# Moving the copy of the transposed attention weights from ScalarE to VectorE, one unit closer to its use

## The reference

```python
x = x + layernorm(attn(layernorm(x), wq, wk, wv, wo))
x = x + layernorm(ffn(layernorm(x), theta, phi, theta_noise, phi_noise))
# attn: 16 heads of 64, window 256; block j of 256 queries sees the keys of
# blocks j-1 and j with  qi + 1 <= ki <= qi + 256, softmax over them, then @ wo.T
# ffn: sqrt((x @ cos(theta + theta_noise))**2 + (x @ sin(phi + phi_noise))**2)
```

## Time and profile before

| what | value |
|---|---|
| median of 3 runs | 4396.93 us (4396.27 to 4718.36) |
| the profiled execution's own time | 4396.27 us |
| its span on the slowest core (core 6) | 4394.7 us (all cores 4368.0 to 4394.7) |
| TensorE busy | 3399.2 us, 77% of the span |
| ScalarE busy | 2266.0 us, 52% |
| VectorE busy | 1429.5 us, 33% |
| mean granted TensorE clock, core 6 | 0.818 |

### The profile page before, as it was taken

The page is one execution under the profiler, slowest core; times in us unless marked ns, Lnnn a source line. Parts: engine busy times, 40 slices in busy tenths (PEclk is TensorE's granted clock), DMA queues, the critical chain, the costliest instruction groups (busy, mean ns, idle before and its releaser), DMA issues.

```text
span 4394.7 us, 51881 instructions; the slowest of 8 cores (4368.0 to 4394.7 us)
## 1 busy us (share of the span) xinstructions
PE 3399.2 (77%) x19680; PEld 2283.5 (52%) x19808; DVE 1429.5 (33%) x3088; ACT 2266.0 (52%) x3200; POOL 111.8 (3%) x215
## 2 busy tenths in 40 slices
PE   0037978889798887979887797978888797888875
PEld 0025645556565555656554555655555565555562
DVE  2312334242433424243342414233241423324142
ACT  3437265372826537282653628274462827446281
POOL 1000000000000000000000000000000000000000
PEclk6566988879798887969788697988879798887978
DMA  6772331405133140513314150422315042241503
GB/s 211 250 250 77 128 122 63 167 29 183 58 129 120 66 164 31 181 58 132 118 70 161 58 191 20 154 96 90 145 53 192 20 154 96 92 147 50 192 10 125
DMA packets 54165, 511.26 MB, mean 116 GB/s; under 512 B 5792, under 2 KB 5920, under 8 KB 28576
## 3 DMA queue, kind: packets, MB, share of 16 engines
q0 software_dynamic: 30384, 266.35, 16.1%
q1 hardware_dynamic: 23536, 241.58, 15.9%
HBM read 465.97 MB, written 41.94 MB: 116 GB/s over the span
## 4 chain that ended last, share of the span: by engine, by line
PE 55%; ACT 24%; issue 9%; DVE 8%; DMA 4%; DVEq 0%; POOL 0%; ACTq 0%; SPq 0%; POOLq 0%
PE pb L516 31%; PE pb L461 16%; ACT L742 11%; ACT L711 4%; ACT attnT_sb L742 4%; PE pb L769 3%; ACT attn_sb L711 3%; DMA wsc<-pl 2%; PE pb L669 1%; DVE stats L697 1%; PE pb L401 1%; DVE ao_sb L807 1%; PE pb L731 1%; DVE attn_sb L700 1%; DVE sc L841 1%
## 5 line engine op out<-in xcount | busy, mean ns | idle before, releaser
L769 PE MATMUL pb<-v_sb,attnT_sb 128*128 128x64 f32 x2880 | 600.1, 365 | 422.5 <-ACT attnT_sb L742 421.5
L769 PEld LDWEIGHTS pb<-v_sb,attnT_sb 128*128 128x128 f32 x2880 | 541.0, 273 | 558.4 <-issue 556.8
L697 DVE TENSOR_REDUCE stats<-pb 128x1 f32<-128x384 f32 (+2 forms) x512 | 269.8, 527 | 1397.6 <-PE pb L669 1397.3
L742 ACT ACT_TABLE_LOAD x512 | 656.9, 1283 | 16.9 <-PE pb L731 8.0
L461 PE MATMUL pb<-fmh,slot0h 128*128 128x256 bf16 x1024 | 280.2, 274 | 264.8 <-DMA slot0l<-wsc 264.8
L414 ACT ACT_TABLE_LOAD x32 | 41.1, 1283 | 793.0 <-PE pb L401 793.0
L711 ACT ACT_TABLE_LOAD x256 | 328.4, 1283 | 99.2 <-DVE attn_sb L700 95.3
L516 PE MATMUL pb<-slot2h,fmh 128*128 128x512 bf16 x961 | 364.2, 379 | 14.2 <-ACT ao_sb L898 13.4
L516 PE MATMUL pb<-slot2l,fmh 128*128 128x512 bf16 x976 | 369.9, 379 | 1.6
L516 PE MATMUL pb<-slot2h,fml 128*128 128x512 bf16 x977 | 370.3, 379 | 0.8
L731 PE MATMUL pb<-eyef_s,attn_sb 128*128 128x128 f32 x1440 | 345.6, 364 | 0.8 <-ACT attn_sb L711 0.8
(11 more groups left out here) (115 smaller groups left out, 4939.1 us busy)
## 6 DMA issues: line engine op xcount, KB each, us to landing
slot0h<-wsc SPq DMA_DIRECT2D x33, 2048.0 KB, 11.3
slot1h<-wsc SPq DMA_DIRECT2D x33, 2048.0 KB, 12.8
slot0l<-wsc POOLq DMA_DIRECT2D x33, 2048.0 KB, 14.0
slot1l<-wsc POOLq DMA_DIRECT2D x33, 2048.0 KB, 15.0
slot2h<-wsc SPq DMA_DIRECT2D x33, 2048.0 KB, 12.2
slot2l<-wsc POOLq DMA_DIRECT2D x33, 2048.0 KB, 14.4
x_sb<-x POOLq DMA_DIRECT2D x32, 512.0 KB, 6.1
y<-sc POOLq DMA_DIRECT2D x32, 512.0 KB, 3.4
```

The lines of the kernel that those rows point to most:

```text
L697: ev[f"mx_{g}_{uu}"] = ve.inc(vector.reduce_max(stats[:, P + up:P + up + 1], kept, axis=AX.X))
L742: ev[f"te_{g}_{u}"] = ac.inc(scalar.activation(attnT_sb[:, upT * SL:upT * SL + nc_], pb[tp_bank][:, 0:nc_], AF.Copy))
L769: ins = tensor.matmul(pb[b_av][:, (h % 8) * DH:(h % 8 + 1) * DH], lhsT, rhs, start=(first_in_bank and ci == 0), stop=(last_in_bank and ci ...
```

## The change

The copy of line 742 goes from ScalarE (`activation` with Copy) to VectorE (`tensor_copy`), the waits on it and the guard of the PSUM bank go from the counter `ac` to `ve`, and the product of a unit is emitted four steps after its scores, not five, ahead of the transposes of the next unit.

```diff
-                @block.scalar
-                def _(scalar, u=u, upT=upT, tp_bank=tp_bank, cs=cs):
-                    kb.wait(scalar, mm, ev[f"tp_{g}_{u}"])
+                @block.vector
+                def _(vector, u=u, upT=upT, tp_bank=tp_bank, cs=cs):
+                    kb.wait(vector, mm, ev[f"tp_{g}_{u}"])
                     nc_ = len(cs) * 128
-                    ev[f"te_{g}_{u}"] = ac.inc(scalar.activation(
+                    ev[f"te_{g}_{u}"] = ve.inc(vector.tensor_copy(
                         attnT_sb[:, upT * SL:upT * SL + nc_],
-                        pb[tp_bank][:, 0:nc_], AF.Copy))
-                kb.bank_set([tp_bank], [(ac, ac.v)])
+                        pb[tp_bank][:, 0:nc_]))
+                kb.bank_set([tp_bank], [(ve, ve.v)])
...
-                    kb.wait(tensor, ac, ev[f"te_{g}_{u}"])
+                    kb.wait(tensor, ve, ev[f"te_{g}_{u}"])
...
-            for u in range(nu + 5):
-                if 0 <= u - 5 < nu:
-                    unit_av(u - 5, *units[u - 5])
+            for u in range(nu + 4):
+                if 0 <= u - 4 < nu:
+                    unit_av(u - 4, *units[u - 4])
```

## The result

The changed kernel is slower: 7.5% by the ratio to the kernel before, 1.0751 with a 95% interval of 1.0736 to 1.0767. Its undisturbed executions took 4721.7 to 4732.1 us, the profiled one 4732.1 us (span 4730.5) against 4396.3 us before; the median over all 12 executions, 4904.5 us, holds eight that a slower state of the chip had disturbed and isn't used. The forecast was 4673 us, in a range of 4535 to 4740.

What follows compares the result with a forecast made beforehand. ScalarE was taken to set the pace at 6.04 us a pair; afterwards a TensorE-VectorE loop would. Fourteen full stages +295 us and two small ones -18 made +277 on 4396.3: 4673 us, range 4535 to 4740.

Steps and rivals of the forecast that it cites:

- ScalarE loses its 512 loads, keeps 256, and is no bound: Attention stages: line 742's table loads go, line 711's stay; ScalarE keeps 1.28 us load, about 1.1 us exponentials a pair.
- The loop product, scores, four instructions, copy, product: TensorE and VectorE wait in turn, maximum and scaling ahead of the copy: 5.67 us a pair full clock, 7.54 half.
- The clock decides, where it was harmless: TensorE's clock sets the pair after the change, 5.67 or 7.54 us; before it was 6.04 us at either level.
- First part +11.7: Full stage up to unit 14's maximum: five loops at 7.54 us plus the previous block's tail on VectorE, 11.7 us later.
- End: no difference: Stage end, from unit 30's maximum to the second division's end: both divisions follow the last copy, no difference taken.
- Second part +9.4: Full stage, unit 14's to unit 30's maximum: eight loops at 6.96 us are 55.7 us against 46.3, +9.4.
- a step at 25% takes 1/(0.25/5.67 + 0.75/7.54) = 6.96 us: Second part: one loop per pair, with 25% at full clock (5.67 us) and the rest at half (7.54 us).
- half clock all through: Rival: stages stay at half clock, second part +14 us, first +11.7; 4738 us, chance 0.09.
- The small stages -18: Two stages with smaller units, first block of each sequence: shorter pairs gain, the ninth block's tail costs; both together -18 us.
- The rival of kept shares: Full clock stays at 27% of the first part and 54% of the second; +149 us, 4545 us, chance 0.20.
- The loop isn't there: Rival: the product finds its copy done, TensorE's own work sets the pace; time not above 4397 us, chance 0.03.
- the gain wins: Rival: TensorE stays at full clock as a 5.67 us loop packs its work more densely; 4311 us, chance 0.06.

Runs made afterwards that it cites:

- e1_ve_five: The changed kernel with the product back at five steps behind its scores, copy still on VectorE: 3959 us, ratio to the kernel before 0.9019.
- e2_act_four: The kernel before with only the order changed, product at four steps and copy still on ScalarE: 5494 and 5450 us on the slowest core.
- e3_filler: The changed kernel with four extra, unneeded products on TensorE ahead of the product at even steps: 4449 us, ratio to the kernel before 1.0114.
- e4_tail_odd: The changed kernel with the tail's four pieces at steps 3, 7, 11, 13 instead of 2, 6, 10, 12, behind the copy: 4577 us.

## Why the prediction was right, point by point

- *ScalarE loses its 512 loads, keeps 256, and is no bound.* Shown by the groups above.
- *The loop product, scores, four instructions, copy, product.* Shown by e1_ve_five and e2_act_four: the order makes it on both engines and its removal opens it. 7.58 us measured at half clock for 7.54, and 5.57 at full for 5.67. The copy took 0.55 us, the middle of my two ends.
- *The clock decides, where it was harmless.* That it decides in the changed kernel is shown by e3_filler. That it was harmless before is shown for the second parts, by the stretches of 6.04 us at either level in the trace of the kernel before; for the first parts it is argued from them.
- *First part +11.7, all of the tail on the loop.* +11.9; e4_tail_odd shows the tail's share. The clock under this term was wrong: I had next to none of it at the full clock, and it was 31% (0.66 in the mean of the 14). It didn't shorten the part, as TensorE stood idle in 66% of that time. That the number fits so well is partly luck.
- *End: no difference.* +0.6. The divisions one after the other are there at 994.01 and 997.43, as said.
- *Second part +9.4.* +12.3. This is the term that was mis-sized, and its failed step is "a step at 25% takes 1/(0.25/5.67 + 0.75/7.54) = 6.96 us". A step took 7.44 us. The share was right (24% in the mean of the 14), but the working spreads it evenly over the loop, and 88% of it fell on the pause and on the work beside VectorE. The step made the part 3.8 us too short; the base of 46.3 us, read off one stage between two maxima, was 0.95 us short of the mean and gave that much back. The 2.9 us left are, on 14 stages, 41 of the 59 us between forecast and profiled execution. The rival "half clock all through" (4738 us) was in effect the better case, though the clock wasn't half all through.
- *The small stages -18.* -13.5.

The rival of kept shares (4545) fell: the share at the full clock in the second parts went from 47% (0.73) to 24%. "The loop isn't there" fell, as TensorE waits for the copy in every pair of the second parts, and "the gain wins" too. The case for this last one had said that a shorter loop packs TensorE more densely; what happened is that the pauses merged into one per pair, at the wrong end.

## What to carry to other kernels

Before an operation is moved to a less busy engine, write down what stands ahead of it on the new queue and follow it until it closes on itself: a copy of 0.55 us that is queued behind work of the next pair, while its reader stands ahead of that pair's scores, cost 773 us; one more step of distance made the same move a gain of 10%. On such a loop side work belongs directly behind the instruction that the other engine waits for. And a mean clock says little by itself: look at which instructions ran at which level before weighting a loop with it.

## What I had not expected of the hardware

TensorE's full clock can be granted and wasted: 22% of the second part at 2.4 GHz, and 7.44 us a pair instead of the 7.58 measured at half clock, because the rise came with the pause (966.20 to 970.00: clock 0.95, TensorE busy for 1.75 of 3.80 us). The opposite is as striking: 4 extra products a pair brought the second part's window from 0.61 to 0.99 and made needless work pay 283 us, with a pause of 1.40 us left in each pair. In the kernel before, four such products raised the mean only from 0.73 to 0.79, where TensorE pauses more than once in a pair (0.62 and 1.87 us in the earlier trace rows); why it rose so much less there wasn't tried.
